# Attention over a Gram matrix of the keys, and weights split at their first use, in a two-layer attention and feed-forward kernel

## The reference

```
x = x + gat(ctx, layernorm(x))                 # graph attention, 8 heads, two layers
x = x + moe(layernorm(x))                      # 8 experts, top 2, silu(g)*u, down
x = x + xattn(layernorm(x), ctx)               # p = layernorm(x)
    kv = ctx @ W_k.T + b_k                     # 512 keys x 128
    out = p @ kv                               # 512 x 128
    sim = out @ kv.T / sqrt(512)
    sim = (sim - mean(sim)) * rsqrt(var(sim) + 1e-6) * gamma + beta     # over the 512 keys
    x = x + softmax(sim)
x = x + ffn(layernorm(x))                      # 512 -> 2048, silu(g)*u, keep 2 of every 4, 2048 -> 512
```

## Time and profile before

| | us |
|---|---|
| median of 3 runs (1054.09 to 1061.31) | 1055.85 |
| profiled execution, its own time | 1056.58 |
| its span, first to last instruction | 1054.8 |
| PE busy | 953.1 (90%) |
| DVE busy | 649.3 (62%) |
| ACT busy | 388.2 (37%) |
| POOL busy | 358.1 (34%) |
| mean granted TensorE clock | 0.958 of 2.4 GHz |

### The profile page before, as it was taken

How to read it: one execution, slowest core, us unless ns; L and a number is a source line. 1 busy time by engine, 2 the same in 40 slices (tenths; PEclk the granted TensorE clock), 3 DMA queues, 4 the chain that set the end, 5 groups by cost and what they waited for, 6 DMA issues and landing times.

```text
span 1054.8 us, 14952 instructions
## 1 busy us (share of the span) xinstructions
PE 953.1 (90%) x4628; PEld 796.5 (76%) x4628; DVE 649.3 (62%) x1441; ACT 388.2 (37%) x682; POOL 358.1 (34%) x439
## 2 busy tenths in 40 slices
PE   4996719999998989947999999999999999999997
PEld 3873418888988878835778888888888888888885
DVE  7986754342242544484695895776858957665446
ACT  4876234443453543332343332432333324222121
POOL 0466024575566665542141221321211211101120
PEclk8998859999999999976999999999999999999999
DMA  8478119887788864355457334475172642545551
GB/s 340 157 148 225 56 46 366 292 300 279 253 312 308 291 231 145 109 183 166 160 163 236 101 100 160 164 231 164 40 240 104 216 160 80 166 154 163 195 160 41
DMA packets 68801, 195.26 MB, mean 185 GB/s; under 512 B 8161, under 2 KB 8289, under 8 KB 67489
## 3 DMA queue, kind: packets, MB, share of 16 engines
q0 software_dynamic: 41392, 129.78, 38.8%
q1 hardware_dynamic: 27312, 64.34, 17.2%
HBM read 146.12 MB, written 50.60 MB: 186 GB/s over the span
## 4 chain that ended last, share of the span: by engine, by line
PE 68%; DVE 7%; DMA 3%; issue 3%; POOL 2%; ACT 2%; DVEq 0%; ACTq 0%; POOLq 0%
PE ps L78 22%; PE ps L79 21%; PE ps L80 21%; DMA w_scratch<-pre 3%; POOL dn_w_lo L1576 1%; PE ps L1626 1%; PE ps L1958 1%; PE ps L1651 1%; DVE gu_w_lo L1801 1%; DVE raw L2558 1%; POOL pre L1582 1%; DVE raw L2574 1%; PE ps L2154 0%; DVE logits L2244 0%; DVE dn_w_hi L1832 0%
## 5 line engine op out<-in xcount | busy, mean ns | idle before, releaser
L78 PE MATMUL ps<-f_x_lo,f_w 128*128 128x512 f32 x512 | 200.9, 392 | 3.2 <-DVE raw L1443 1.8
L79 PE MATMUL ps<-f_x_hi,f_w 128*128 128x512 f32 x512 | 200.2, 391 | 0.0
L80 PE MATMUL ps<-f_x_hi,f_w 128*128 128x512 f32 x512 | 200.1, 391 | 0.0
L1437 ACT ACTIVATE moe_rows<-ps 128x512 f32<-128x512 f32 x64 | 38.1, 596 | 227.7 <-PE ps L80 227.7
L1443 DVE TENSOR_TENSOR raw<-moe_rows,ps 128x512 f32<-128x512 f32 x64 | 43.9, 686 | 126.1 <-PE ps L80 118.5
L78 PEld LDWEIGHTS ps<-f_x_lo,f_w 128*128 128x128 f32 x512 | 96.7, 189 | 24.0 <-issue 2.1
L78 PE MATMUL ps<-gu_w_lo,m_xT_hi 128*128 (+1 forms) x312 | 105.3, 338 | 9.3 <-issue 6.4
L80 PEld LDWEIGHTS ps<-f_x_hi,f_w 128*128 128x128 f32 x512 | 96.7, 189 | 20.2
L79 PEld LDWEIGHTS ps<-f_x_hi,f_w 128*128 128x128 f32 x512 | 96.7, 189 | 19.9
L78 PE MATMUL ps<-f_w,kv_c_hi 128*128 128x512 f32 x256 | 102.4, 400 | 2.3 <-DVE x L2593 2.3
L79 PE MATMUL ps<-f_w,kv_c_lo 128*128 128x512 f32 x256 | 101.7, 397 | 0.0
(11 more groups left out here) (350 smaller groups left out, 1975.6 us busy)
## 6 DMA issues: line engine op xcount, KB each, us to landing
f_w<-w_scratch POOLq DMA_DIRECT2D x52, 1024.0 KB, 5.7
f_w<-w_scratch POOLq DMA_DIRECT2D x52, 512.0 KB, 5.5
w_scratch<-pre POOLq DMA_DIRECT2D x32, 768.0 KB, 5.0
pre_raw<-in_ffn SPq DMA_DIRECT2D x32, 384.0 KB, 6.4
raw<-in_moe_gu SPq DMA_DIRECT2D x32, 352.0 KB, 4.3
y_scratch<-m_y SPq DMA_DIRECT2D x39, 256.0 KB, 3.4
raw<-in_moe_dn SPq DMA_DIRECT2D x24, 256.0 KB, 4.5
x<-in_x SPq DMA_DIRECT2D x4, 1024.0 KB, 10.9
```

The source lines that it names most:

```text
L78: eng.matmul(out, lhs_hi, rhs_lo, start=start, stop=False)
L79: eng.matmul(out, lhs_lo, rhs_hi, start=False, stop=False)
L80: return eng.matmul(out, lhs_hi, rhs_hi, start=False, stop=stop)
L1437: act.activation(sg[:, k % 2, :], self.gate_bank(n, r), ACT.Silu).then_inc(self.silu, 1)
```

## The change

- **Experts.** Only quarter 0 is split in this stage: 8 chunks instead of 32, one in every third block (loads at blocks 3m, splits at 3m+6). Key 0 is now centred by DVE (mean over the 512 keys subtracted) before it is turned, and its straight copy is multiplied by gamma at block 35 and split at block 36. gamma is loaded early for this.
- **Adding the experts' outputs.** For tiles 0 and 1 both outputs are added by GpSimd; DVE adds the second one only for tiles 2 and 3.
- **First attention.** PE makes the Gram matrix G of the centred keys (128x128), then G·out. The variance of a row of scores is out·(G·out)/512: DVE multiplies, PE sums the 128 partitions with a one-column product, DVE adds epsilon. The mean is zero. `centre` (4 times `bn_stats`, `bn_aggr`, subtract and multiply by gamma) is gone, `scores` reads PSUM. ACT makes a further copy of `out` in each half.
- **First gate and up products by halves.** As soon as tiles 0 and 1 are turned, PE does the half with tokens 0 to 255 of gate and up r = 0, after the turns of tiles 2 and 3 that of gate r = 1; then the other halves.
- **Feed-forward weights.** Quarters 1 to 3 are split at their first use, in 18 pieces of 1024 columns (12 of gate and up, 6 of down): SP loads raw values into one of three stages, ACT rounds into `w_hi`, GpSimd subtracts into `w_lo`, PE waits for that (`raw_lo`) in place of the fetch, and SP stores hi and lo into `w_scratch` for the later uses.

Of the diff, the core:

```
-CHUNKS, CW = 2 * Q * RQ, 3 * D // 2
+CHUNKS, CW = 2 * RQ, 3 * D // 2
+FRESH = tuple(range(1, Q))
...
+    def pieces(n, slot):
+        down = (("down", n - 1, slot - 1),) if n - 1 in FRESH and slot <= RQ // 2 else ()
+        gate_up = (("gate_up", n + 1, slot - 1),) if n + 1 in FRESH else ()
+        return down + gate_up
...
+    def load_piece(self, sp, piece):
+        kind, s, i = piece
+        at, t = self.place[piece], RQ * QUARTER[s]
+        if at >= 3:
+            sp.wait_ge(self.raw_lo, at - 2)
...
+    def act_piece(self, act, piece):
+        kind, s, i = piece
+        at, stage = self.place[piece], self.piece_stage(piece)
+        act.wait_ge(self.raw_got[at % 3], 16 * (at // 3) + 16)
+        if kind == "gate_up":
+            act.wait_ge(self.products, RQ * (FIRST[s] - 1) + i + 1)
+            if s >= 2:
+                act.wait_ge(self.kept_gu[i], 16 * (s - 1))
+            act.copy(self.w_hi[i][:, 0:2, :], stage).then_inc(self.raw_hi, 1)
...
+    def pool_piece(self, pool, piece):
+        pool.wait_ge(self.raw_hi, self.place[piece] + 1)
+        if kind == "gate_up":
+            pool.tensor_tensor(self.w_lo[i][:, 0:2, :], stage, self.w_hi[i][:, 0:2, :].bitcast(F32), ALU.subtract
+                               ).then_inc(self.raw_lo, 1)
...
+        LOADS, SPLITS = ({3 * m + at: m for m in range(CHUNKS)} for at in (3, 6))
...
-                if g <= CHUNKS:
-                    chunk_hi(j, i)
+                if g in SPLITS:
+                    chunk_hi(SPLITS[g])
...
+        pe.wait_ge(e["kv_lo_done"], B)
+        gram()
         turn(0, 0)
         turn(0, 1)
         pe.wait_ge(e["y_done"], REAL + 2)
         turn(0, 2)
         turn(0, 3)
         context(0)
+        gram_context(0)
         similar(0)
+        sums(0)
+        similar(1)
         context(1)
-        similar(1)
-        for t in range(TB):
-            turn(1, t)
+        gram_context(1)
+        similar(2)
+        sums(1)
+        similar(3)
+        turn(1, 0)
+        turn(1, 1)
+        pe.wait_ge(self.lo_done[1], 2)
+        pe.wait_ge(u.got_gu[0], 16)
+        gate_up_half(0, 0, 0)
+        gate_up_half(0, 1, 0)
+        turn(1, 2)
+        turn(1, 3)
+        pe.wait_ge(u.got_gu[1], 16)
+        gate_up_half(1, 0, 0)
         pe.wait_ge(self.lo_done[1], TB)
-        u.pe_gate_up(pe, 0, 0)
+        gate_up_half(0, 0, 1).then_inc(u.gates, 1)
+        gate_up_half(0, 1, 1).then_inc(u.products, 1)
+        gate_up_half(1, 0, 1).then_inc(u.gates, 1)
...
-        add(0)
-        add(1)
         stats(0, 0)
+        gram_lo()
         add(2)
         add(3)
         stats(0, 1)
...
         o_lo(0)
+        squares(0)
         dve.wait_ge(self.ld_row, 32)
-        centre(0)
-        centre(1)
+        variance(0)
         scores(0)
         o_lo(1)
         scores(1)
+        squares(1)
         prob(0)
-        centre(2)
+        variance(1)
         prob(1)
-        centre(3)
         stats(1, 0)
         scores(2)
         scores(3)
...
             first.act(act)
             for r in range(1, RQ):
                 early(r)
                 u.act_silu(act, 0, r - 1, sg)
                 late(r)
+                if r >= 2:
+                    split_pieces(0, r - 1)
```

More of the change, by code:

```diff
@@ L1367, in __init__ @@
         self.acc_done, self.acc_free = sem(tag + "acc_done"), sem(tag + "acc_free")
+        self.raw = outer["dram"]["ffn"]
+        self.stage = [outer["raw"][:, 4 * D:6 * D]] + [outer["fresh_raw"][:, k, :] for k in range(2)]
+        self.raw_got = [sem(f"{tag}raw_got{k}") for k in range(3)]
+        self.raw_hi, self.raw_lo = sem(tag + "raw_hi"), sem(tag + "raw_lo")
+        self.kept_gu, self.kept_dn = ([sem(f"{tag}kept_{name}{r}") for r in range(RQ)] for name in ("gu", "dn"))
+        self.place = {}
@@ new lines, in __init__, with piece_stage @@
+        for n in range(UNITS):
+            for slot in range(1, RQ + 1):
+                for piece in self.pieces(n, slot):
+                    self.place[piece] = len(self.place)
+    @staticmethod
+    def pieces(n, slot):
+        down = (("down", n - 1, slot - 1),) if n - 1 in FRESH and slot <= RQ // 2 else ()
+        gate_up = (("gate_up", n + 1, slot - 1),) if n + 1 in FRESH else ()
+        return down + gate_up
+    def piece_stage(self, piece):
+        return self.stage[self.place[piece] % 3].rearrange("p (k n) -> p k n", k=2)
@@ new lines, in loads, with wait_gate_up, wait_down @@
+    @staticmethod
+    def loads(s):
+        return s + 1 - sum(f <= s for f in FRESH)
+    def wait_gate_up(self, pe, n, r):
+        s = SPLIT[n]
+        if s in FRESH:
+            pe.wait_ge(self.raw_lo, self.place["gate_up", s, r] + 1)
+        else:
+            pe.wait_ge(self.got_gu[r], 16 * self.loads(s))
+    def wait_down(self, pe, n, r):
+        s = SPLIT[n]
+        if s in FRESH:
+            pe.wait_ge(self.raw_lo, self.place["down", s, r // 2] + 1)
+        elif self.down_at(n) == 2:
+            pe.wait_ge(self.got_dn[r], 16 * self.loads(s))
+        else:
+            pe.wait_ge(self.got_last[r], 16)
@@ L1642, in key_turn @@
             def key_turn(b):
-                pe.wait_ge(kvT_made, b + 1)
+                if b == 0:
+                    pe.wait_ge(centred, 1)
+                else:
+                    pe.wait_ge(kvT_made, b + 1)
                 for i in range(TB):
@@ L2492, in round_hid, with split_pieces @@
                     act.copy(hid_hi[:, r, :], hid[:, r, :]).then_inc(u.hid_hi_done, 1)
+            def split_pieces(n, slot):
+                for piece in u.pieces(n, slot):
+                    u.act_piece(act, piece)
             first.act(act)
```

288 lines of the change are left out of this document (203 added, 85 removed).

## The result

The changed kernel takes 1059.54 us (median of 20 runs, 1058.16 to 1062.88), the one before 1054.24 beside it (20 runs, 1049.83 to 1061.31): ratio 1.005, 95% interval 1.0036 to 1.0063. It is 5 us slower, where 23 us less were forecast. The profiled execution has a span of 1058.8 us and took 1060.53.

A forecast was written before the change was run, and what follows sets the result against it. PE was taken as the bound almost everywhere, falling short in the experts and in the first attention, where DVE's chain bounds. -17 - 3 - 5.5 + 1.5 = -24 from 1056.58 us profiled gave 1032.5 us; 1024 to 1039 got 0.68.

The forecast's parts named there:

- Experts, -17: Experts: with 24 of 32 chunks gone, waits for chunk stores vanish and blocks take 6.7 us; gain 12.5 to 19.5 us.
- Rival B: Experts: the stalls come with the change of expert, not the chunks; gain -4 instead of -17, 1045.6 us; chance 0.09 with mixtures.
- issue gaps: Experts: 6.4 us of PE waits called "issue", for which the profile shows no cause; counted as half gone.
- First attention, -3: First attention: variance from the Gram matrix brings the last norm at about 479.4 us against 482.52.
- halves, -5.5: First gate and up products: half run while DVE makes tiles 2 and 3; -5.5 us, bounds -3 to -7.
- That case: First products: turns of tiles 2 and 3 stand behind the low-clock halves, so the products end at 488.6, not 487.7.
- The table load: First attention: ACT's table load of 1.28 us, hidden before, stands ahead of the first exponential; 1.1 us put on that wait.
- Feed-forward, +1.5 for the pieces: Feed-forward: splitting 18 pieces lies beside PE's work, except for GpSimd blocking DVE; +1.5 us, bounds 0 and +9.
- Rival C: Feed-forward: PE waits for pieces late by a whole subtraction, 18 x 2.4 = 43 us, net +17.5, 1074 us; chance 0.05.
- The lock: Feed-forward: a DVE instruction with two SBUF inputs is blocked while GpSimd reads SBUF; 2158 ns against 682 ns in the rows.
- rival A: Feed-forward, units 0 to 3: DVE, blocked by GpSimd's pieces, falls behind; +9 instead of +1.5, 1040 us; chance 0.15.

The follow-up runs named there:

- e9: The kernel before, unchanged, profiled in the place where the later experiments run: span of 1053.2 us.
- e10: The changed kernel, unchanged, timed again beside the later experiments: 1060.03 us, ratio 1.0069 to the kernel before.
- e4: Changed kernel with 32 chunks in the experts and whole weight fetches again, so only the new attention, adding and halves stay: 1053.07 us, ratio 0.993 to before.
- e1: Also called the ceiling: changed kernel with no pieces, every quarter using quarter 0's weights, fetched whole: 1037.78 us, ratio 0.9781 to the kernel before.
- e5: Changed kernel with GpSimd's pieces ahead of the attention's small steps and a fourth buffer for raw pieces: 1046.59 us, ratio 0.9852 to the kernel before.
- e2: Changed kernel with GpSimd taking each piece ahead of the next slot's small attention steps, from unit 1 on: 1054.18 us, ratio 0.9943 to the kernel before.
- e12: Same kernel as e5, timed again in one place with e13: 1041.52 us, ratio 0.9872 to the kernel before.
- e13: As e5, but GpSimd fills the low parts with zeros for about as long, without reading SBUF: 1034.18 us, ratio 0.9805 to the kernel before.
- the first two groups: The first eight follow-up runs, made on two of four chips; the kernel before has medians of 1060.3 and 1061.0 us beside them.

## Why the prediction was wrong

**Experts, -17: right.** The last copy comes 18.45 us sooner, in the first pair of profiles and in e9 and e10 (counted from the first copy, 18.3 and 15.8). The cause was mostly the chunks: with 32 of them back (e4) five waits of ACT for a store are back. Their number alone is worth 10.3 us by the profiles of e4 and e1 and 15 to 16 by the ratios, so a few of the 18 may be from the other edits in this stage; that wasn't taken apart. Rival B (-4) is out. Half of the issue gaps went, as assumed (6.4 to 3.4).

**First attention, -3, and halves, -5.5: right, somewhat too large.** Together 6.5 us of the forecast 8.5 in the changed kernel, 5.2 in e4 alone and 8.1 from e9 to e10; this stretch differs by 3 us among the profiles with the new attention (43.9 to 47.2), so the single numbers carry little. The stretch from the last copy to the last norm shrank by 2.0 (34.1 to 32.1), where 3 were put. The first halves all ran at the low level, 0.21 us a product of 256 columns, until 466.1; the turns of tiles 2 and 3 stood behind them until 464.94, while the norm that they turn began at 462.09 and took 1.0. That case was named (488.6 instead of 487.7); it cost up to 1.8 us. The table load came where it was put, in front of the first exponential.

**Feed-forward, +1.5 for the pieces: the step that failed.** It measured +28.9, against an upper bound of 9. The term took PE's wait for the pieces to be covered by slack; it left out what stands ahead of a piece, and behind it, in the queues of ACT, GpSimd and DVE. Three of its sentences were wrong.

- "Behind ACT's wait for a raw load stands the next silu ... I find ACT held up to 4 us there, and PE's three banks allow for that." ACT was held 6.96 us, and what was behind it on ACT was not only a silu but the rounding of the attention's turned tile, which has no banks in front of it. The load was counted by the DMA's mean share and not by when its buffer came free, nor by the full queues that it then met: issued at 557.90, it let ACT go at 563.44, with a DMA share of 0.97 from 560 on. A fourth buffer took the wait away (e5, 6 us of the last stretch).
- "A down piece is done about 4 us before slot 4 of its unit." That counts ACT and GpSimd as free when the piece comes. GpSimd stood 5.55 us at a small step of the attention that waits for DVE, with the piece behind it in order. Moving two lines was worth 15 us of the last stretch (e2; 11 by the ratios). Rival C named exactly this queue and gave it 0.05; its price was 43 us if each of 18 pieces were late by 2.4. In fact PE waited for one piece of GpSimd, by 7.7 us, and for one rounding behind a late load, by 6.4, and each stall also took the clock.
- "Bounds 0 and +9, taken: +1.5, near the low end, since most of DVE's hidden steps read PSUM." The hidden steps do, and weren't held. The tests around them (L2778, L2794) read SBUF twice and were held up to 3.6 us a group, and the hidden step stands behind them on DVE. The lock costs 7.3 us (e12 against e13), near rival A's +9.

The row that the lock's price came from was also read loosely. 2158 ns is the mean of one instruction of 2.89 us and three of 1.91 or 1.92; here is one of these with GpSimd's beside it, in the kernel before:

```profile
387.76 1.91 DVE L1826 TENSOR_TENSOR kv_c_lo<-kv_c_raw,kv_c_hi 128x512 fp32r<-128x512 f32 x1 [2.06 <-ACT kv_c_hi L1749]
```

```profile
387.29 1.83 POOL L1582 TENSOR_TENSOR pre<-pre_raw,pre 128x768 fp32r<-128x768 f32 x1 [4.76 <-ACT pre L1766]
```

DVE's starts within GpSimd's and ends 0.55 us after it, about its own plain length (0.68). So here DVE lost what was left of GpSimd's instruction; 2158 ns isn't its length.

The order change, the fourth buffer and the lock are worth 15 + 6 + 7 us of the last stretch, each in the order in which they were taken out; the last 3.7 (e13 against the ceiling) weren't taken apart. Together that is 32, where the changed kernel stands 30 over the ceiling: single profiles don't add up better than that. And the sum priced no clock: the waits cost two fifths more than their length (8 on 20.5).

## What to carry to other kernels

- Slack of a new step is to be taken from the queue of each engine it goes through, in order: what stands ahead of it and for whom that waits. A mean busy share of 0.3 says nothing on that: here one small step of GpSimd that waited for DVE cost PE 7.7 us, with GpSimd busy 52.2 of the 150 us from 500 on.
- Where PE is full, a stall is paid with its length and then with the clock behind it. Waits of 20.5 us more came to 29.
- Before giving GpSimd a large SBUF subtraction, list what DVE does beside it that has two SBUF inputs, and who stands behind that, not which steps PE waits for directly. And try the cheap mending, order and one more buffer, before judging the idea: the change was 0.5% slower as it stood and 1.3 to 1.5% faster with both (e12, e5).

## What was not expected of the hardware

- The clock after short stalls: 0.72 over the 10 us behind a wait of 4.26, 0.75 behind one of 6.42 and 0.83 behind one of 7.74, and 0.83 behind the one of 3.96 at 505.48, where before the window from 500 to 650 ran at 1.00. In these four the loss doesn't grow with the length of the wait.
- A block of the experts that takes 13.4 to 14.6 us in the eight profiles of the first two groups and 7.5 in the other nine, of e1:

```profile
405.95 0.59 ACT L1825 COPY m_y<-ps 128x512 f32<-128x512 f32 x1 [1.49 <-PE ps L81]
411.87 0.46 ACT L1812 ACTIVATE m_sg<-ps 128x352 f32<-128x352 f32 x1 [5.34 <-DMA xn_scratch<-g_xn]
...
420.08 0.59 ACT L1825 COPY m_y<-ps 128x512 f32<-128x512 f32 x1 [3.25 <-PE ps L81]
```

ACT's silu starts 5.3 us late, though PE's gate product for it was done at 407.9. The named releaser is a DMA of a much earlier stage, so it isn't the cause. In those places before was 5 to 9 us slower as well (1060.3 and 1061.0 against 1052.0 and 1055.1), which fits a delay of 6.5 us in every kernel, but before was not profiled there. The cause stays open.
- A fill of GpSimd of 1024 columns takes 0.96 us and a subtraction of as many 2.4 (DVE's takes 1.22): replacing one by the other tests two things at once.
